# A decoder layer on one core: earlier latent products, value transposes moved, key copies moved, and a latent output product of 99 rows

## The reference, cut to what matters

```python
x = x + latent_attention(layernorm(x))          # 16 batches of 128 tokens, 256 columns
x = x + grouped_cross_attention(layernorm(x), ctx, ctx, mask)
x = x + experts(layernorm(x))                   # 32 experts, top 8, cut at a sum of 0.8

# latent attention
c  = (x @ W_to_kv.T) @ W_compress.T             # 32 columns
ch = layernorm(c) * ln_gamma + ln_beta
q, k, v = ch @ W_q_comp.T, *split(ch @ W_kv_comp.T)
o  = softmax(causal(rope(q) @ rope(k).T / sqrt(32))) @ v
z  = o @ W_comp2lat.T
out = z @ W_to_kv + z @ W_out_res.T + b_out_res
```

## Time and profile before

| | us |
|---|---|
| runs shown | 516.5, 516.7, 511.64 |
| median | 516.5 |
| the profiled execution's own time | 512.39 |
| its span, first to last instruction | 510.5 |

### The profile page before, as it was taken

One profiled execution on the slowest core, in us unless ns is written; L12 is line 12 of the kernel. 1 busy time (PEld: TensorE's weight loads), 2 busy tenths in 40 slices (PEclk: granted clock), 3 DMA queues, 4 the chain that ended last, 5 costly groups with the idle time before them and its releaser, 6 DMA issues.

```text
span 510.5 us, 12310 instructions
## 1 busy us (share of the span) xinstructions
PE 454.5 (89%) x3120; PEld 389.1 (76%) x3120; DVE 378.2 (74%) x1854; ACT 317.9 (62%) x869; POOL 327.5 (64%) x473
## 2 busy tenths in 40 slices
PE   3689999999999999999978999989999999999920
PEld 2467787787787787777756998879999999888910
DVE  4356788888877888877896885655565667999886
ACT  2477778777778777778735555556565656555520
POOL 4112167777767777777667777777676767665770
PEclk9999999999999999999999999999999999999985
DMA  6331447862232232322128679999655679998785
GB/s 191 110 133 54 166 141 207 232 175 87 95 104 93 94 116 79 104 92 76 62 87 257 200 251 312 294 295 290 209 156 147 203 216 316 339 351 305 256 276 178
DMA packets 52261, 93.79 MB, mean 184 GB/s; under 512 B 9974, under 2 KB 41246, under 8 KB 52002
## 3 DMA queue, kind: packets, MB, share of 16 engines
q1 hardware_dynamic: 37346, 46.11, 31.2%
q0 software_dynamic: 12240, 32.14, 16.8%
q10 hardware_dynamic: 2608, 14.76, 8.7%
HBM read 53.61 MB, written 43.41 MB: 190 GB/s over the span
## 4 chain that ended last, share of the span: by engine, by line
PE 52%; DVE 21%; DMA 8%; issue 6%; ACT 5%; SPq 4%; POOL 2%; POOLq 0%; ACTq 0%; DVEq 0%
PE bank L1411 11%; PE bank L1443 7%; DVE NM L789 7%; PE bank L1104 5%; DVE NM L791 4%; PE bank L1362 4%; PE bank L1245 4%; PE bank L1287 3%; PE bank L1261 3%; DMA qN<-rows 2%; PE bank L1433 2%; PE bank L1166 2%; SPq L361 2%; PE bank L1099 2%; DMA KA<-parts 2%
## 5 line engine op out<-in xcount | busy, mean ns | idle before, releaser
L469 POOL DMA_INDIRECT rows<-rowb,idx x112 | 110.8, 989 | 55.1 <-DVE rowb L889 28.4
L1411 PE MATMUL bank<-wgu_sb,PT 128*128 x572 | 105.0, 327 | 0.7 <-ACT PT L496 0.7
L1411 PEld LDWEIGHTS bank<-wgu_sb,PT 128*128 128x128 f32 x572 | 91.3, 190 | 0.8 <-issue 0.8
L479 POOL DMA_INDIRECT parts<-PT,dst_all x72 | 71.4, 991 | 29.4 <-issue 21.9
L496 ACT ACTIVATE PT<-bank 128x512 f32<-128x512 f32 x108 | 61.4, 593 | 28.1 <-PE bank L1443 19.3
L1443 PE MATMUL bank<-wd_sb,VC 96*128 x286 | 73.6, 379 | 0.0
L589 ACT ACTIVATE PT<-bank 128x512 f32<-128x512 f32 x96 | 53.7, 621 | 4.7 <-PE bank L1261 4.6
L1443 PEld LDWEIGHTS bank<-wd_sb,VC 96*128 96x128 f32 x286 | 52.2, 190 | 4.0
L998 DVE SCALAR_TENSOR_TENSOR PT<-PT,bank 128x192 f32<-128x192 f32 x72 | 25.2, 350 | 40.0 <-ACT PT L623 39.8
L623 ACT ACTIVATE PT<-bank 128x192 f32<-128x192 f32 x72 | 23.7, 329 | 45.2 <-PE bank L1411 45.2
L496 ACT ACTIVATE Q<-bank 9x256 fp32r<-9x256 f32 (+1 forms) x96 | 42.5, 443 | 11.3 <-PE bank L1240 9.6
(11 more groups left out here) (270 smaller groups left out, 1141.8 us busy)
## 6 DMA issues: line engine op xcount, KB each, us to landing
pool_a<-rows SPq DMA_DIRECT2D x96, 148.5 KB
qN<-rows SPq DMA_DIRECT2D x47, 148.5 KB
wgu_sb<-wgu_d SPq DMA_DIRECT2D x8, 768.0 KB, 4.9
rows<-pad SPq DMA_DIRECT2D x33, 152.0 KB
pool_a<-parts ACTq DMA_DIRECT2D x5, 896.0 KB, 6.5
KA<-parts ACTq DMA_DIRECT2D x5, 896.0 KB
Q<-parts ACTq DMA_DIRECT2D x5, 896.0 KB, 7.0
wd_sb<-wd_d SPq DMA_DIRECT2D x2, 1536.0 KB
```

The source lines that it names most:

```text
L469: gp.indirect_dma_start(out=rows, out_offset=bass.IndirectOffsetOnAxis(ap=idx[b % 2][:, k:k + 1], axis=0), in_=rowb[b % 2][:, :], in_offse ...
L479: gp.indirect_dma_start(out=parts, out_offset=bass.IndirectOffsetOnAxis(ap=dst[q % NDST][:, j:j + 1], axis=0), in_=yb[q % FEED][:, j, :], ...
L1411: last = t.matmul(GU_PS[q % 2][:, j * 2 * NI:(j + 1) * 2 * NI], xTb[q % 2][:, j, k * P:(k + 1) * P], wgu_sb[:, k, one_of(expert[i]), :].sq ...
```

## The change

The order tables get new due times, and these steps get new contents:

- v is written three times side by side (96 columns, `VW` 66 becomes 99), the weight of the output product stands three times in `wback` (high part, low part, high part, and three rows for the bias), and o transposed comes as high part and low part: ACT copies 99 rows, and a new step `r12` of DVE subtracts to get 33 rows of low part. `r13` is then one f32r product with a contraction of 99 rows in place of an f32 one of 128 rows. Set-up: three folded products in place of one, two copies by ACT, a new step `wb` of DVE (three instructions, once), a bias load in three rows.
- `r17b` writes to a bank of the ring in place of `R_PS`, and so no longer waits for the copy of the first half.
- ACT's step `kv` is split: the key copy (`kh`) comes first, DVE takes the low part of the keys at once, and the value copies (`kva`) wait for DVE.
- `po` is split: its last two instructions become `px`. `g5`, `g6` and `px` move about 11 us later, next to `g7`; `n3` moves before them and before `r5`.
- POOL's `r7` moves from behind `sc1` and `xT` to right behind `sc0`. ACT's `r12` moves ahead of `kT`. PE's `r7` and `r8` move ahead of `lg` and `r17`, `vt` and `r17b` ahead of `kv`, `rk` to the end, `oT` behind `mx3`. SP's `n3` moves behind the next load of x.

The diff, cut to its core:

```diff
-VW = 66
+VW = 3 * DC + 3
...
-    "PE": {"r4": -3.9, "r6": 0.5, "r7": 3.5, "kv": 5.8, "r8": 6.8, "r9": 7.9, "r11": 9.9, "r12": 11.9, "kT": 11.0, "r13": 15.3,
+    "PE": {"r4": -3.9, "r6": 0.5, "r7": 1.7, "kv": 5.8, "r8": 3, "r9": 5.9, "r11": 9.7, "r12": 10.9, "kT": 11.0, "r13": 14.9,
...
-    "ACT": {"mk": -7, "r7": 5.7, "kv": 6.3, "r8": 7.3, "r10": 8.2, "r11": 9.3, "r12": 12, "kT": 11.5, "r15": 18.9, "r16": 21.4,
+    "ACT": {"mk": -7, "r7": 3.95, "kv": 5.93, "kva": 5.94, "r8": 4.6, "r10": 5.95, "r11": 9.8, "r12": 11.2, "kT": 11.5, "r15": 18.9, "r16": 21.4,
...
-            "vt": 43.5, "wo": 51.8, "n3": 55.7, "g1": 58.7, "g2": 60.6, "g3": 61.3, "g4": 61.5, "g5": 61.8, "g6": 62.1,
-           "po": 62.9, "g7": 64, "g8": 73.7, "g9": 74.2, "g10": 75.2, "g11": 75.4, "g12": 75.6, "g13": 75.8, "la1": 77.4 + (SEEN - 1) * PERIOD,
+            "vt": 42.9, "wo": 51.8, "n3": 53.6, "g1": 58.7, "g2": 60.6, "g3": 61.3, "g4": 61.5, "g5": 72.4, "g6": 72.45,
+           "po": 62.9, "px": 72.6, "g7": 73, "g8": 73.7, "g9": 74.2, "g10": 75.2, "g11": 75.4, "g12": 75.6, "g13": 75.8, "la1": 77.4 + (SEEN - 1) * PERIOD,
...
-    "POOL": {"r1": -12, "r4": -2.2, "r7": 3.9, "r13": 17.4, "kL": 29.5, "r17": 46.3, "wo": 51.5, "xT": 60, "sc0": 74.6, "sc1": 77.4, "sc2": 80.5,
+    "POOL": {"r1": -12, "r4": -2.2, "r7": 2.3, "r13": 17.4, "kL": 29.5, "r17": 46.3, "wo": 51.5, "xT": 60, "sc0": 74.6, "sc1": 77.4, "sc2": 80.5,
-    "SP": {"ldx": -6.0, "ldc": -2.0, "n3": 42.5, **{f"w{n}": 25.0 + 12.0 * n for n in range(10)}}}
+    "SP": {"ldx": -6.0, "ldc": -2.0, "n3": 54, **{f"w{n}": 25.0 + 12.0 * n for n in range(10)}}}
...
-                copy(v_sb[b % 2][:, 0:DC], R_PS[b % 2][:, 4 * DC:5 * DC]).then_inc(S["v_sb"], 1)
+                copy(v_sb[b % 2][:, 0:3 * DC].rearrange("p (t c) -> p t c", t=3), R_PS[b % 2][:, 4 * DC:5 * DC].unsqueeze(1).to_broadcast([P, 3, DC])).then_inc(S["v_sb"], 1)
...
-                copy(oT_sb[b % 2][0:DC + 1, :], R_PS[b % 2][0:DC + 1, 0:P]).then_inc(S["oT_sb"], 1)
+                copy(oT_sb[b % 2][0:VW, :], R_PS[b % 2][0:VW, 0:P]).then_inc(S["oT_sb"], 1)
...
-                copy(kN3[b % 2][:, :, 0:3:2, :], o[:, 0:GD].rearrange("p (f c) -> p f c", f=2).unsqueeze(2).to_broadcast([P, 2, 2, QR]))
+                copy(kN3[b % 2][:, :, 0:3:2, :], o[:, 0:GD].rearrange("p (f c) -> p f c", f=2).unsqueeze(2).to_broadcast([P, 2, 2, QR])).then_inc(S["kh"], 1)
+
+            def kva(b):
+                o = ring_bank("kv", b)
+                act.wait_ge(S["klo"], nth("klo", b))
...
+            def r12(b):
+                low = slice(2 * DC, 3 * DC + 1)
+                dve.wait_ge(S["oT_sb"], nth("oT_sb", b))
+                v.tensor_tensor(oT_sb[b % 2][low, :], R_PS[b % 2][low, 0:P], oT_sb[b % 2][low, :].bitcast(f32), ALU.subtract).then_inc(S["ol"], 1)
...
-                dve.wait_ge(S["va"], nth("va", b))
+                dve.wait_ge(S["kh"], nth("kh", b))
...
+            def px(b):
                 dve.wait_ge(S["pt"], nth("pt", b))
...
-                pe.wait_ge(S["oT_sb"], nth("oT_sb", b))
-                t.matmul(R_PS[b % 2][:, 0:D], oT_sb[b % 2][:, :], wback[:, :], start=True, stop=True).then_inc(S["o1"], 1)
+                pe.wait_ge(S["ol"], nth("ol", b))
+                t.matmul(R_PS[b % 2][:, 0:D], oT_sb[b % 2][0:VW, :], wback[0:VW, :], start=True, stop=True).then_inc(S["o1"], 1)
...
-                    else:
-                        pe.wait_ge(S["Q2"], nth("Q2", b, 1))
+                    o = ring("r17b", b) if hf else R_PS[b % 2]
```

More of the change, by code:

```diff
@@ L98 @@
 ENDING = [(s, NB - 1) for s in ("oT", "wo", "xT", "lg", "rk")]
-READ = {"kv": ("klo", 1), "kT": ("KA", 1), **{f"mx{u}": ("rmax", u + 1) for u in range(6)}, "c": ("Q3c", 2),
+READ = {"r17b": ("Q2", 2), "kv": ("va", 1), "kT": ("KA", 1), **{f"mx{u}": ("rmax", u + 1) for u in range(6)}, "c": ("Q3c", 2),
         **{f"s{i}": ("e", i + 1) for i in range(6)}, "vt": ("on", 1),
@@ L175, in decoder_kernel @@
         nmax, den, rden = ([one(), one()] for _ in range(3))
-        prob, probT, oT_sb = (two(n, [P, P]) for n in ("prob", "probT", "oT_sb"))
+        prob, probT = (two(n, [P, P]) for n in ("prob", "probT"))
+        oT_sb = two("oT_sb", [P, P], f32r)
         qN = two("qN", [P, HG * 2, 3, QR], f32r)
@@ L385, in _ @@
                 gp.memset(chT[p][:, :], 0.0).then_inc(S["setup_g"], 1)
-                gp.memset(v_sb[p][:, DC:], 1.0).then_inc(S["setup_g"], 1)
+                gp.memset(v_sb[p][:, 3 * DC:], 1.0).then_inc(S["setup_g"], 1)
             for p in range(2):
                 gp.memset(qkT[p][:, :, :], 0.0).then_inc(S["setup_g"], 1)
-                gp.memset(oT_sb[p][:, :], 0.0).then_inc(S["setup_g"], 1)
+                gp.memset(oT_sb[p][:, :].bitcast(f32), 0.0).then_inc(S["setup_g"], 1)
             gp.memset(NM[:, :, :], 1.0).then_inc(S["setup_g"], 1)
@@ L517, in r8 @@
                     act.wait_ge(S["setup_p"], 2)
-                    copy(wback[0:DC, :], V_PS[0:DC, 0:D]).then_inc(S["folded"], 1)
+                    copy(wback[0:3 * DC, :], V_PS[0:3 * DC, 0:D]).then_inc(S["folded"], 1)
+                    act.wait_ge(S["w_small"], 5 * 16)
+                    copy(wback[3 * DC:VW, :], bout_sb).then_inc(S["folded"], 1)
             def r10(b):
@@ L546, in f @@
                         act.wait_ge(S["s"], nth("s", b - 2, 6))
-                    copy(Q2[b % 2][0:CR, hf, :, :, :], R_PS[b % 2][0:CR, :].rearrange("p (h a n) -> p a h n", h=HG, a=2)).then_inc(S["Q2"], 1)
+                    o = ring_bank("r17b", b) if hf else R_PS[b % 2]
+                    copy(Q2[b % 2][0:CR, hf, :, :, :], o[0:CR, :].rearrange("p (h a n) -> p a h n", h=HG, a=2)).then_inc(S["Q2"], 1)
                 return f
@@ L674, in _ @@
                       "mk": mk, "r7": r7, "r8": r8, "r10": r10, "r11": r11, "r12": r12, "r15": r15, "r16": r16, "r17": q_rows(0), "r17b": q_rows(1),
-                      "kv": kv, "kT": kT, "c": c, **{f"s{i}": s_(i) for i in range(6)}, "pv1": pv,
+                      "kv": kv, "kva": kva, "kT": kT, "c": c, **{f"s{i}": s_(i) for i in range(6)}, "pv1": pv,
                       "oT": oT_, "xT": xT, "g1": g1})
@@ L1039, in pl @@
                 v.tensor_copy(tbl_i[:, PADS_AT:], END_PS[:, 96:96 + NE]).then_inc(S["lists"], 1)
-            schedule("DVE", {"la1": la1, "la2": la2, "la3": la3, "mi": mi, "mk": mk, "r1": r1, "r4": r4, "r5": r5, "r6": r6, "r7": r7, "r9": r9, "r10": r10, "r13": r13, "wqc": wq_centred, "r16": r16,
+            schedule("DVE", {"la1": la1, "la2": la2, "la3": la3, "mi": mi, "mk": mk, "r1": r1, "r4": r4, "r5": r5, "r6": r6, "r7": r7, "r9": r9, "r10": r10, "r12": r12, "wb": wb, "r13": r13, "wqc": wq_centred, "r16": r16,
                       "kv": kv, **{f"mx{u}": mx(u) for u in range(6)}, "vt": on, "wo": wo_, "n3": n3,
                       "g1": g1, "g2": g2, "g3": g3, "g4": g4, "g5": g5, **{f"g{6 + n}": sums(n) for n in range(3)}, "g9": g9, "g10": g10, "g11": g11,
-                      "g12": g12, "g13": g13, "po": po, "cn": cn, "pl": pl,
+                      "g12": g12, "g13": g13, "po": po, "px": px, "cn": cn, "pl": pl,
                              **{f"me{q}": lambda _, q=q: meta(q) for q in range(EARLY + 1)}, **{f"ab{q}": lambda _, q=q: ab(q) for q in range(EARLY + 1)}})
@@ L1127, in r4 @@
                     pe.wait_ge(S["setup_v"], 5)
-                    t.matmul(V_PS[0:DC, 0:D], l_c2l, l_outres, start=True, stop=True).then_inc(S["setup_p"], 1)
+                    for n in range(3):
+                        last = t.matmul(V_PS[n * DC:(n + 1) * DC, 0:D], l_c2l, l_outres, start=True, stop=True)
+                    last.then_inc(S["setup_p"], 1)
             def r6(b):
@@ L1189, in f @@
                         pe.wait_ge(S["ql"], nth("ql", b))
-                    else:
-                        pe.wait_ge(S["Q2"], nth("Q2", b, 1))
+                    o = ring("r17b", b) if hf else R_PS[b % 2]
                     for h in range(HG):
-                        last = t.matmul(R_PS[b % 2][0:CR, h * P:(h + 1) * P], qN[b % 2][:, 2 * h + hf, :, :].rearrange("p a c -> p (a c)"), identr[:, :], start=True, stop=True)
+                        last = t.matmul(o[0:CR, h * P:(h + 1) * P], qN[b % 2][:, 2 * h + hf, :, :].rearrange("p a c -> p (a c)"), identr[:, :], start=True, stop=True)
                     last.then_inc(S["qT"], 1)
```

26 lines of the change are left out of this document (17 added, 9 removed), and 10 rows, old and new, of tables (AT, names).

## The result

The changed kernel takes 521.32 us (median of four runs, 519.92 to 523.51), the kernel before beside it 514.07: a ratio of 1.0157, interval 1.0103 to 1.0211. The change makes the kernel slower. The profiled execution has a span of 519.5 where the one before had 510.5, so 9.0 us are to be found; the medians lie 7.3 apart, since the profiled execution before was 1.7 under the median beside it. The sum in the prediction said +0.1, and the range ended at 521.

What follows compares the result with a forecast made beforehand. A main chain over PE, ACT and DVE bounds the kernel, a POOL-DVE loop 2% below it would pace it afterwards. -1.8 - 2.9 + 2.9 + 1.9 = +0.1 on 512.4; between two run levels it named 514.2 us, range 506 to 521.

Steps and rivals of the forecast that it cites:

- the start: Set-up to batch 0's maxima: these start 1.8 us sooner, with bounds of -0.5 and -2.5.
- the last stretch: Last slots and end: PE's wait in la1 costs +1.3, later scatters of batch 12 +0.6, together +1.9 us.
- The steady slot: Maxima of batch 3 to those of batch 14: 15.71 us a slot against 15.31, +2.9 over 11 slots.
- DVE's wait before n3: Sign that the forecast is right: DVE idle some 0.8 us before n3, released by the transfer of `rows`.
- POOL's wait before sc0: Sign that the forecast is right: POOL idle over 2.5 us before sc0.
- The landing's bounds: Time from sc6's end until its scatter has landed and n3 can start: 1.53 us, bounds 1.4 to 1.6.
- the landing stretches: Rival, chance 0.17: x's loads slow sc6's landing to 1.9 us, slot 16.11, +4.8 in all, 517.2 us.
- la1: Last slots: PE waits in la1 for batch 12's counts from g5, now behind n3: +1.3 us.
- The first three slots: Slots before any scatter: -0.7, -1.7 and -0.5 us, together -2.9.
- The stall at the load of batch 4: Second slot: a 1.9 us stall on DVE goes, with SP's n3 behind the load; the slot gains 1.7.
- The main chain: Waits through a slot over PE, ACT's `qkT` copy and DVE's maxima: 15.31 to 14.7 us; ruling alone, chance 0.08, 500.4.
- The rival without the landing: Rival, chance 0.20: the landing doesn't hold n3, r5 waits for POOL, slot 15.20, -6.4 in all, 506.0 us.

Runs made afterwards that it cites:

- e3: The changed kernel with 20 extra 1 x 1 products on PE in its idle time at the very start: 520.41 us, ratio 1.0128 to the kernel before.
- e7: e2 with the output product as before: f32, 128 rows, v written once, no r12 or wb on DVE: 505.58 us, ratio 0.9825 to the kernel before.
- e8: e6 with ACT's two copies of the folded weight moved behind the exponential of batch 0: 505.20 us, ratio 0.9827 to the kernel before.
- e1: The changed kernel with n3 alone put back on DVE, behind g9 and r5: 514.51 us, ratio 1.0032 to the kernel before.
- e2: The changed kernel with three buffers of rowb and idx in place of two, and three scatter semaphores: 507.14 us, ratio 0.9848 to the kernel before.
- e4: The changed kernel with g5 of batch 12 alone at its old place on DVE: 515.58 us, ratio 1.0056 to the kernel before.
- e6: The changed kernel with the edits of e2 and e5 together: 504.66 us, ratio 0.9774 to the kernel before.
- e5: The changed kernel with g5, g6 and g7 moved behind g4 on DVE, two row buffers: 508.45 us, ratio 0.9862 to the kernel before.
- e11: e6 with px moved ahead of r5 on DVE: 501.13 us, ratio 0.9758 to the kernel before.
- e10: The kernel before with SP's n3 alone moved behind the load of x for batch 4: 514.54 us, ratio 1.0005.
- e12: e6 with POOL's r4 ahead of its wo and DVE's r5 ahead of n3: 505.68 us, ratio 0.9863 to the kernel before.

## Why the prediction was wrong, step by step

Three terms of the sum were mis-sized: the start (by 1.9), the landing in the late slots (by 2.4) and the last stretch (by 3.5). With 1.0 from the other rows these are the 8.9 between +0.1 and +9.0.

- **The steady slot was right.** 15.71 by the sum, 15.64 measured. In the slot shown: sc0 at 162.65 to the end of sc6 at 172.89 is 10.24 (sum 10.45), to n3 1.60 (1.53), n3 to r5 0.82 (0.68), r5 to the end of g13 2.17 (2.17), to sc0 0.88 (0.88). The landing read from SP's one wait, 2.47 after the start, is 2.55 to 2.61 here; the estimate of 2.36 worked out from the Trainium skill ("DMA: Bandwidth & Descriptors", section "Anatomy of one DMA") lies 0.2 below. DVE's wait before n3 was 0.4, not 0.8, since DVE itself came to n3 later; POOL's wait before sc0, 3.0, was as foreseen.
- **The landing's bounds, 1.4 to 1.6, failed.** They came from one row, and twelve waits of n3 hang on that term. In four of them the landing took 2.3 to 2.9 after the end of sc6. The rival "the landing stretches" named the effect and not the cause: in every slot the packets of x's loads begin only behind the scatter's, and there are none left in the last two late slots (SP's last load of x is at 221.39). The cause is the transfers of instructions, which e3 moved. This is 2.4 of the missing 8.9 us.
- **la1 was foreseen and undersized.** Priced at +1.3 as a wait of PE, it is 1.21 in e3, where the landing ahead of it is on time, and 1.94 in the changed kernel, where that landing is 0.7 late. The slot grew by 4.5: behind the wait the granted clock was 0.50 for 3.4, and again later for some 6. The whole last stretch is +5.45 where the sum had +1.9. That a stalled PE can come back at half rate stood nowhere in the sum.
- **The start, -1.8, failed in the profile.** Two terms were wrong. The two added folded products cost nothing (six rows in 1.07, where two took 1.06); their +0.6 was also added up wrongly, since three times 1.06 from 8.36 on ends at 11.5 and not at 11.1. But the exponential of batch 0 went from 15.70 to 17.01: 0.67 of that is already there at the first product of r7 (12.19 for 11.52; the first load landed 0.37 later and DVE's set-up copies took longer), the rest is ACT's second copy of the weight and the handshake of keys and values. The rest of the start can't be told apart from one execution to another: in nine profiles with the changed start (e7 and e8 alter it) the first c comes between 31.58 and 34.18, mean 32.6, in three with the old start at 33.19, 33.87 and 34.56. A good part of that is when TensorE's rate doubles: the four products of the first r16 took 1.08 before, and 2.05, 1.80, 1.88, 1.32 and 1.10 in the changed kernel, e1, e2, e4 and e6. So the gain is about 1, within the bounds that the prediction gave, and a single profile carries 1.3 either way: that the changed kernel's shows none is in part bad luck.
- **The first three slots, -2.9, came to -2.0.** The stall at the load of batch 4 went as foreseen; the third slot gained nothing (15.16 for 15.19) until g5 to g7 were moved in e5 and e6 (14.78). So the g steps, moved late, already stood on its path; the chain of waits there runs over them and sc0, as in e2.
- **The main chain** was put at 14.7, and e11, with the other limits out of its way, has 14.75. That is in part luck: the savings on the `qkT` path and the cost of r12 made the sum, and e11's chain runs over neither.
- **The rival without the landing** was put at 15.20; e2, which is this case, has 15.11. That is luck too: the 15.20 waits in r5 for POOL, which e2 does not.

What stays open: why the granted clock falls in the last slot of some executions and not of others. Behind a wait of PE for the maxima there it falls for 3.4 in e4 (the wait is 1.64) and in e10 (1.63), and stays at 1.00 in the kernel before (1.63) and in e12 (2.17); so this later fall is not the change's own. Open as well is which engine's instructions q14 carries.

## What to carry to other kernels

Before a step is moved ahead, look at which buffer it writes and which transfer must have landed first: here the landing cost 0.5 a slot, and a third row buffer turned the change from 1.6% slower into 1.5% faster. A term that comes from one row and counts twelve times needs the spread of that row. A step that another engine's chain waits for (here POOL's r7) carries everything that is put ahead of it in its stream. And a stall of PE outside its steady stretch is to be priced with the products that follow it, which may run at half clock, as here behind 1.94.

## What the runs showed of the hardware

A transfer of instructions delays a scatter: 2.55 to 2.61 from its start to n3 without one, up to 3.84 with one, in 60 slots of five kernels. The queue q8 brings 28 such packets in the whole run, 0.46 MB or 16 KB each. The Trainium skill says in "Runtime: NRT & Kernel Launch", section "Instruction fetch mechanics", that instructions are fetched in blocks of 16 KiB, 256 instructions each, over a DMA queue; the packet size agrees, and so does e3, where 80 more PE instructions (40 products and 40 weight loads in the trace) moved the packets. In "DMA: Bandwidth & Descriptors", section "Queues, rings and completion order", it says that a semaphore's increment lands only after every earlier write of that DMA engine, across its queues; the late landings agree with it, but need no such rule, since the scatter's own packets are late. Queues of the changed kernel from 2.12 after the start of the scatter to n3, first the steady slot (171.93), then the late one (236.73):

```profile
q1 hardware_dynamic: 8, 0.01, 10.3%
```

```profile
q0 software_dynamic: 5, 0.01, 2.6%
```

Of the scatter's 96 packets none is left to begin in the steady slot, and five in the late one. They begin one behind the other, the last ending 3.11 after the start of the scatter, as they would on one engine that the packet of 16 KB held; which engine carried a packet the trace doesn't tell.
